# Values of two attention units issued back to back in a two-layer fused attention kernel

## The reference

```python
x = x + layer0(_gn(x), ...)   # global attention with relative position biases
x = x + layer1(_gn(x), ...)   # 7 x 7 neighbourhood attention plus 16 register keys
# layer 0, S = 1024, head width 16
attn_bias = rel_h[:, :, :, :, None] + rel_w[:, :, :, None, :]
scores = q @ k^T * SCALE + attn_bias
out = softmax(scores) @ v, then @ w_proj.T + b_proj
# layer 1
scores = where(mask_cat, q @ k_cat^T * scale, -1e30)
out = softmax(scores) @ v_cat, then @ out_w.T + out_b
```

## Time and profile before

| what | value |
|---|---|
| median of 3 runs | 4923.62 us (4919.65 to 4926.85) |
| profiled execution, its own time | 4917.51 us |
| its span | 4915.8 us |
| TensorE busy (matmul) | 4495.7 us, 91% |
| VectorE busy | 3081.0 us, 63% |
| ScalarE busy | 2606.4 us, 53% |
| GpSimd busy | 892.4 us, 18% |
| mean granted TensorE clock | 0.952 of 2.4 GHz |
| one global stage, 1917.7 to 2071.4 us | 153.7 us, clock 0.99 |
| the local stage behind it, 2099.7 to 2183.6 us | 83.9 us, clock 0.88 |

### The profile page before, as it was taken

One profiled execution on the slowest core, in us unless ns is written; L12 is line 12 of the kernel. 1 busy time (PEld: TensorE's weight loads), 2 busy tenths in 40 slices (PEclk: granted clock), 3 DMA queues, 4 the chain that ended last, 5 costly groups with the idle time before them and its releaser, 6 DMA issues.

```text
span 4915.8 us, 97560 instructions
## 1 busy us (share of the span) xinstructions
PE 4495.7 (91%) x32598; PEld 2289.2 (47%) x32598; DVE 3081.0 (63%) x5558; ACT 2606.4 (53%) x3955; POOL 892.4 (18%) x1899
## 2 busy tenths in 40 slices
PE   3979999999999999999999999999999999999998
PEld 2334453544535455454544535445453544535444
DVE  2736657566675656657566675656657566675644
ACT  1443646555564555646555564555646555565564
POOL 3122021122102212021122102212021121102111
PEclk7887999999999999999999999999999999999998
DMA  6333253432424433244432424434144432424401
GB/s 122 85 68 75 47 109 76 99 79 59 95 56 99 94 71 85 44 106 80 99 79 55 93 62 99 94 69 88 44 108 79 99 79 52 96 62 99 87 14 39
DMA packets 235881, 386.25 MB, mean 79 GB/s; under 512 B 58396, under 2 KB 133728, under 8 KB 235360
## 3 DMA queue, kind: packets, MB, share of 16 engines
q1 hardware_dynamic: 189280, 266.13, 23.7%
q10 hardware_dynamic: 21504, 75.51, 7.7%
q0 software_dynamic: 24576, 37.80, 4.8%
HBM read 227.79 MB, written 88.08 MB: 64 GB/s over the span
## 4 chain that ended last, share of the span: by engine, by line
PE 74%; DVE 10%; issue 5%; DMA 4%; SPq 4%; ACT 2%; DVEq 0%; POOL 0%; ACTq 0%
PE P L1123 14%; PE P L1141 14%; PE P L1085 13%; PE P L948 7%; PE P L949 6%; DVE mx L891 6%; PE P L1061 5%; PE P L1173 4%; PE P L1194 4%; PE P L1093 3%; DMA QA<-queries 2%; DVE mxc L897 1%; PE P L1166 1%; DMA biases<-xn 1%; PE P L1211 1%
## 5 line engine op out<-in xcount | busy, mean ns | idle before, releaser
L891 DVE TENSOR_REDUCE mx<-P 128x1 f32<-128x512 f32 x3072 | 1924.0, 683 | 436.3 <-PE P L1085 432.9
L761 ACT ACTIVATE probs<-P 128x1024 f32<-128x1024 f32 x1536 | 1507.0, 1022 | 781.3 <-PE P L1141 780.8
L1085 PE MATMUL P<-K,AR 96*128 96x256 f16 x6144 | 1100.0, 283 | 15.4 <-DVE mx L891 6.2
L1141 PE MATMUL P<-AR,K 113*128 113x512 f16 x3072 | 921.8, 382 | 4.1 <-DMA AR<-mrow 2.9
L897 DVE TENSOR_REDUCE mxc<-P 128x1 f32<-128x336 f32 (+1 forms) x1536 | 649.4, 475 | 307.9 <-PE P L1094 304.4
L777 ACT ACTIVATE probs<-P 128x320 f32<-128x320 f32 (+3 forms) x1632 | 617.2, 436 | 411.3 <-PE P L1194 334.5
L1123 PE MATMUL P<-probs,V 128*17 128x512 f32 x6144 | 811.8, 600 | 9.9 <-ACT probs L761 9.9
L1085 PEld LDWEIGHTS P<-K,AR 96*128 96x128 f16 x6144 | 540.4, 99 | 546.7 <-DVE mx L891 209.5
L1141 PEld LDWEIGHTS P<-AR,K 113*128 113x128 f16 x3072 | 216.1, 98 | 662.8 <-ACT probs L761 520.4
L1194 PE MATMUL P<-A,K 113*128 113x320 f16 (+2 forms) x1536 | 444.5, 305 | 13.6 <-ACT probs L777 12.8
L1093 PE MATMUL P<-K,A 112*128 112x320 f16 (+1 forms) x1536 | 403.4, 298 | 53.8 <-DVE mx L891 36.4
(11 more groups left out here) (120 smaller groups left out, 3704.2 us busy)
## 6 DMA issues: line engine op xcount, KB each, us to landing
AR<-biases SPq DMA_DIRECT2D x384, 256.0 KB, 7.8
AR<-queries ACTq DMA_DIRECT2D x96, 512.0 KB, 5.8
biases<-xn SPq DMA_DIRECT2D x192, 256.0 KB, 3.0
AR<-queries ACTq DMA_DIRECT2D x96, 256.0 KB, 8.5
K<-oraw POOLq DMA_DIRECT2D x384, 64.0 KB, 4.8
xin<-in_x_dram SPq DMA_DIRECT2D x16, 768.0 KB, 10.5
queries<-oraw SPq DMA_DIRECT2D x384, 32.0 KB, 4.8
QA<-queries SPq DMA_DIRECT2D x192, 64.0 KB, 5.2
```

What stands on the lines that cost most here:

```text
L761: nc.scalar.activation(probs[:, u % RING, j:j + 2, :], P[:, b:b + 2, :], ACT.Exp).then_inc(p_done[0], 1)
L891: V_.reduce_max(mx[:, n // 2, n % 2:n % 2 + 1], bank, AX.X).then_inc(used, 1)
L1085: last = mm(bank[:, QD * (v % 2):QD * (v % 2) + QD], AR[0:ROWS_MAX[0], part % SLOTS, v, c, j, 128 * q:128 * q + 128], K0[0:ROWS_MAX[0], h, ...
L1141: last = mm(P[:, j, :], K0[0:ROWS, h, 128 * kt:128 * kt + 128], AR[0:ROWS, p % SLOTS, kt // 2, :, j, :], start=True, stop=True)
```

## The change

In the global layer, TensorE now issues no values after an even unit, and after an odd unit u those of u-1 and of u. In the local layer the same is done by a unit's place u in its group: after u = 1 the register unit's values (u = 0), after u = 2, 4, 6 and 8 the values of u-1 and of u. All waits inside `use` stay, and so do scores, jobs and their places; the other engines' programs are the same.

```diff
@@ attend_global
                         run_jobs(after[step], 0)
-                    if u:
+                    if u % 2:
                         use(u - 1)
-                use(UNITS[0] - 1)
+                        use(u)
                 jobs_read(after)
@@ attend_local
                     ends.append(step)
-                    if full:
+                    if u == 1:
                         use(full - 1)
-                use(UNITS[1] - 1)
+                    elif u and u % 2 == 0:
+                        use(full - 1)
+                        use(full)
                 jobs_read(after)
```

## The result

The changed kernel takes 5081.2 us (median of 4 runs, 5079.5 to 5082.0), the kernel before 4924.7 us in the same runs: a ratio of 1.0316, 95% interval 1.0301 to 1.0332, or 156 us more. The forecast was 5087, the range 5000 to 5150.

A forecast was written before the change was run, and what follows sets the result against it. TensorE's queue, 74% of the chain, was taken as the bound; 113 us global, 46 local and 7 for the last two images' local stages make 166 us more, giving 5087 us, between 5083.5 and 5089.6; range 5000 to 5150.

The forecast's parts named there:

- (a) The saving: Global values on TensorE: a second set issued right behind a first costs 0.86 us in place of 0.98.
- (b) VectorE's ring: Dense global pairs: two value sets outlast three job banks; VectorE idles 1.29 us per pair, period 6.17 against 5.83.
- (c) ScalarE's circle: Global pairs: values wait for the last exp and hold up the scores ScalarE needs; a pair takes 5.57 us.
- One sign named in advance: Values' idle time before ScalarE staying near its 10 us for the whole run would show the prediction wrong.
- the two phase starts: Global layer, pairs where ScalarE also copies the output: 0.64 and 0.99 us more, 1.6 together per usual image.
- the pairs of eight local jobs: Global layer, three pairs per usual image: 0.39 us more on 5.18, 1.2 together.
- the seven of eight layer-0 jobs: Global layer, seven dense pairs per usual image with eight layer-0 jobs: 0.34 us more each, 2.4 together.
- The four mixed and bias pairs: Global layer, pairs with mixed or bias jobs, VectorE already idle at every set: 0.1 us more each, 0.4 together.
- The four pairs of key tiles named above: Local layer, units 3 to 6 of second and third group: second set outlasts the job banks' cover, 0.43 us more.
- The gain by saved switches: Rival, both layers: only the saved tiling-mode switches matter, 106 us saved, giving 4812 us; chance 5%.
- The balance: Rival, whole kernel: waits in half the pairs, savings in the rest, about no change, 4924 us; chance 3%.
- the slower clock through ten units per image: Rival: new waits lower TensorE's clock through 10 units per image, 240 us more, 5320 us; chance 4%.

The follow-up runs named there:

- Experiment 2: Two job banks in place of three: the kernel before takes 5563.2 us (1.1304), the changed kernel 5553.0 us (1.1286).
- Experiment 3: Layer-0 maxima over 256 of 512 columns, layer-0 exps of a quarter of the scores: kernel before 4749.1 us, changed kernel 4821.1 us.
- the faster version: Kernel before with each global unit's last job issued behind the values: 4872.1 us; with the maxima's transposes also one step later, 4860.4 us.
- experiment 5: Kernel before with pairs in the global layer only, the last job of each pair between its two sets of values: 5019.3 us (1.0198).

## Why the prediction was right

**(a) The saving.** The second set costs 0.86 us, as taken from the two halves of the local values: 1.91 us busy against 1.05. By starts, the next scores come 1.85 us after the first set where it was 0.98. This holds only where it doesn't wait: with local jobs the second set starts 0.99 us after the first.

**(b) VectorE's ring.** The forecast 1.29 us of idle and 6.17 us of period are measured to the digit. Experiment 2 takes one bank away, and the idle time grows by 0.59 and 0.60 us and the period by 0.60 and 0.63 in the two orders; in the dense global stretch the sign turns. Experiment 3 takes the term away, and the dense pairs of both layers then gain in place of losing. Shown for these pairs.

**(c) ScalarE's circle.** Right in kind, 0.12 us too long: 5.57 forecast, 5.45 measured. The mis-sized term is the row of exps. I took 3.90 us from units in which each exp came late; in a circle where the scores are ready, four take 3.77. With it, 0.64 + 3.77 + 0.05 + 0.98 = 5.44. At the phase start, with the copy, I had 6.17; the values at 2121.17 us and 2127.11 us of the trace are 5.94 apart. Experiment 3 shows that the circle does not depend on the jobs. One sign named in advance would have misled by its letter: the values' idle time before ScalarE did stay near 10 us (12.3) on the matmuls' row. The wait was there, but on the weight loads, 208 us where it was 83.

**The sums.** Global layer +118.5 for a forecast of 113 (usual images 7.0 for 6.7, image 0 12.8 for 13), local layer +47.9 for 53 (usual images 2.8 for 3.3, the last two 8.2 for 7). The usual global stage is closer than its terms are. By pairs, the two phase starts cost 1.19 us together and not 1.6, the pairs of eight local jobs 0.28 and not 0.39, the seven of eight layer-0 jobs 2.0 in all and not 2.4. The four mixed and bias pairs, which I put at 0.4 together, cost 1.8, and nearly all of it is the pair with the bias jobs (+1.87). So a term of 0.1 us that was 1.87 made up for others that were too long: the agreement to 0.3 us per stage is partly luck. The local stage is alike. The four pairs of key tiles named above cost 0.30 to 0.55 us each for a forecast of 0.43, but the first group of heads, with its bias jobs, costs 1.45 of the 2.85 us, 1.29 of it at units 1 and 2, for which there was next to nothing in the sum.

**The rivals.** The gain by saved switches exists, 0.12 us per pair, but it comes through only where neither circle has grown longer than what it replaces: 0.2 us per pair in the dense stretches of experiments 2 and 3. The trace thus agrees with what the Trainium skill, TensorEngine Tiling, Key Properties, says of the drain at a change of mode: one burst in place of two saves 0.12 us; no run separates a drain from other costs of starting a burst. It does not carry the result. The balance did not come. Nor did the slower clock through ten units per image: steps 48 to 75, with most of the dense pairs, kept the full clock in every stage. But the clock did cost something in one unit or two. Of the 1.87 us of the bias pair 1.4 come with it, less 0.2 that the single order had lost in the pair behind; with image 0 that is some 20 of the 156 us, worked out from the pairs above. The forecast had none of it in its sum. It read the half clock there as the normal state of the kernel before, while only 4 of the 16 stages had it.

## What to carry to other kernels

In these runs, two engines joined by a ring of buffers were decoupled only for the ring's depth times the consumer's time per item. In this kernel, grouping work on the producer was paid in full, period by period, beyond that length. So before joining two bursts, add up the path from a buffer coming free, across the burst, to the next item, and compare; if it is over already, try to move an item of the ring behind the burst, as the faster version does. And a group that includes the newest item, here the values of the unit just scored, puts that item's producer into the loop. Last, look for the largest difference by place before trusting a sum that fits: here it stood in a pair that the sum had put at next to nothing.

## What was not expected of the hardware

The granted clock of the global stages is a little lower with pairs. In the windows view, the 15 usual global stages had 0.99 or 1.00 before and 0.97 to 1.00 after. Where the bias jobs had TensorE wait, for 0.77 us as before and now again for 0.47, the clock fell to its lower level, and the next burst of values, now both sets, ran at it:

```profile
1999.47 2.07 PE L1061 MATMUL P<-QA,Z 128*128 128x64 f16 x16
2001.47 3.61 PE L1123 MATMUL P<-probs,V 128*17 128x512 f32 x16
```

3.61 us in place of 1.91: twice the work of the earlier trace rows meets the slow clock. This happened, to the whole burst or a part of it, in 15 of the 16 global stages, and in 14 of them in the run of the global change alone, where the order before had it in 4; with a job between the two sets (experiment 5) it was 4. The waits of 0.43 us inside the dense pairs left the clock alone: it was 1.00 through steps 48 to 75 in all 16 stages.
